# Last local attention of a twelve-layer kernel: order of the last quarter's units, and who multiplies what

## The reference, cut to what matters

```python
def _L3_attn_ref(x, w_qkvw, w_out):
    H = 16; G = 4; DIM = 128; HD = DIM // H // G          # HD = 2
    B, S, dim = x.shape
    qkvw = x @ w_qkvw
    chunks = jnp.split(qkvw, G, axis=-1)
    subs = [jnp.split(t, G, axis=-1) for t in chunks]
    q = jnp.concatenate([subs[i][0] for i in range(4)], axis=0)   # k: [1], v: [2], w: [3]
    ...
    q, k, v = (shp(q), shp(k), shp(v))        # reshape(B*G, H, -1, HD).swapaxes(1, 2)
    w = w.reshape(B * G, H, -1, HD)
    scores = q @ k.swapaxes(-2, -1) * HD ** (-0.5)
    attn = jax.nn.softmax(scores, axis=-1)
    o = (attn @ v).swapaxes(1, 2).reshape(B, S, dim)
    return o * w.reshape(B, S, dim) @ w_out
...
x = x + _L3_attn_ref(_layernorm(x, axis=-1), L3_attn_w_qkvw, L3_attn_w_out)
x = x + _L3_ffn_ref(_layernorm(x, axis=-1), ...)
```

## Time and profile before

| | us |
|---|---|
| median of 3 runs | 2057.41 (2051.45 to 2058.58) |
| profiled execution | 2055.21 |
| its span | 2053.4 |
| TensorE matmul busy | 1747.0 (85%) |
| VectorE busy | 1340.8 (65%) |
| ScalarE busy | 1045.8 (51%) |
| GpSimd busy | 904.9 (44%) |

### The profile page before, as it was taken

One profiled execution on the slowest core, in us unless ns is written; L12 is line 12 of the kernel. 1 busy time (PEld: TensorE's weight loads), 2 busy tenths in 40 slices (PEclk: granted clock), 3 DMA queues, 4 the chain that ended last, 5 costly groups with the idle time before them and its releaser, 6 DMA issues.

```text
span 2053.4 us, 50642 instructions
## 1 busy us (share of the span) xinstructions
PE 1747.0 (85%) x20238; PEld 1177.5 (57%) x20238; DVE 1340.8 (65%) x3578; ACT 1045.8 (51%) x2709; POOL 904.9 (44%) x1088
## 2 busy tenths in 40 slices
PE   7678999999988789998888879999999997447596
PEld 4323556566664555654566656776676764125496
DVE  6799996576675565455672277656877876666622
ACT  4445665487873652224532346666666753115243
POOL 2343554555551523320514152326767578433543
PEclk9878999999999999999978999999999998766598
DMA  9000000100008100034014301000000000040197
GB/s 362 1 1 0 0 1 1 77 5 5 4 5 348 67 4 0 1 153 197 3 68 133 110 22 42 22 22 20 13 25 19 11 12 1 10 155 30 57 308 231
DMA packets 60429, 130.68 MB, mean 64 GB/s; under 512 B 16714, under 2 KB 38941, under 8 KB 54561
## 3 DMA queue, kind: packets, MB, share of 16 engines
q1 hardware_dynamic: 56896, 121.32, 16.5%
q0 software_dynamic: 3296, 6.12, 0.9%
HBM read 107.97 MB, written 20.12 MB: 62 GB/s over the span
## 4 chain that ended last, share of the span: by engine, by line
PE 55%; DVE 20%; issue 9%; ACT 7%; DMA 4%; POOL 4%; SPq 1%; POOLq 1%; DVEq 0%; ACTq 0%
PE PS L3321 4%; PE PS L2516 4%; PE PS L424 3%; PE PS L3368 3%; PE PS L3353 2%; PE PS L3352 2%; DMA arena<-in_ctx 2%; PE PS L3310 2%; PE PS L460 2%; PE PS L1521 2%; PE PS L2316 2%; PE PS L4328 2%; PE PS L4319 2%; PE PS L1497 2%; PE PS L1082 1%
## 5 line engine op out<-in xcount | busy, mean ns | idle before, releaser
L321 POOL TENSOR_TENSOR arena<-arena 128x4 f32<-128x4 f32 (+3 forms) x109 | 118.7, 1089 | 347.4 <-DVE arena L264 225.9
L1655 POOL TENSOR_TENSOR arena<-arena 128x128 f32<-128x128 f32 x448 | 164.4, 404 | 53.0 <-PE PS L1703 15.6
L3436 ACT ACTIVATE arena<-PS,arena 128x289 f32<-128x289 f32 x256 | 127.6, 503 | 73.2 <-DVE arena L3550 72.8
L3550 DVE TENSOR_REDUCE arena<-PS 128x1 f32<-128x289 f32 x256 | 113.5, 454 | 71.9 <-PE PS L3321 67.8
L3321 PE MATMUL PS<-arena 128*128 128x289 f32 x512 | 150.6, 417 | 10.4 <-ACT arena L3436 7.5
L1258 POOL TENSOR_TENSOR arena<-arena 128x512 f32<-128x512 f32 x64 | 83.9, 1311 | 109.8 <-DVE arena L1403 109.8
L1610 ACT COPY arena<-PS 32x128 f32<-32x128 f32 x384 | 99.5, 259 | 21.8 <-PE PS L1511 17.7
L3321 PEld LDWEIGHTS PS<-arena 128*128 128x128 f32 x512 | 87.4, 191 | 34.5 <-ACT arena L3436 16.8
L3279 POOL TENSOR_TENSOR arena<-arena 128x1024 f32<-128x1024 f32 x14 | 33.0, 2355 | 159.8 <-ACT arena L3427 159.8
L3564 DVE TENSOR_TENSOR arena<-PS,arena 128x580 f32<-128x580 f32 x128 | 97.6, 762 | 4.4
L368 PE MATMUL PS<-arena 128*128 128x512 f32 x166 | 89.9, 677 | 9.5 <-DVEq L4635 8.7
(11 more groups left out here) (471 smaller groups left out, 4768.6 us busy)
## 6 DMA issues: line engine op xcount, KB each, us to landing
arena<-in_ctx SPq DMA_DIRECT2D x32, 1091.0 KB, 10.2
arena<-in_f_w SPq DMA_DIRECT2D x39, 514.0 KB, 5.5
arena<-in_ctx SPq DMA_DIRECT2D x16, 834.0 KB, 16.3
lists<-arena SPq DMA_DIRECT2D x8, 1040.0 KB, 10.8
arena<-in_f_w SPq DMA_DIRECT2D x32, 256.0 KB, 2.9
arena<-in_ctx SPq DMA_DIRECT2D x16, 512.0 KB, 3.9
arena<-in_mid SPq DMA_DIRECT2D x1, 3796.5 KB, 12.4
arena<-in_late SPq DMA_DIRECT2D x1, 3204.0 KB, 11.4
```

What stands on the lines that cost most here:

```text
L321: e.tensor_tensor(x, x, half.broadcast_to(list(x.shape)), ALU.pow).then_inc(*T.done("norm_root", tag))
L1655: k = e.tensor_tensor(dst[:, b], spread(src[:, b, :], [P, HG, S], 1), spread(self.g.C["headmask"], [P, HG, S], 2), ALU.mult)
L3436: e.activation(self.weights(n, k, 0, UL), PS[:, self.score_bank(n, k), 0:UL], ACT.Exp, bias=self.st[:, h, k:k + 1], accum_out=self.st[:, h ...
L3550: e.tensor_reduce(self.st[:, n % 2, k:k + 1], PS[:, self.score_bank(n, k), 0:UL], AXX, ALU.max, negate=True).then_inc(*T.done("k3_least", ...
```

## The change

In quarter 3's part and what is interleaved with it:

1. GpSimd issues both end products right after the first two of its six remaining passes; the other four follow them.
2. VectorE issues `products(0)`, `products(1)`, then both residual adds, then the mix of unit 10; the norm statistics of quarters 0 and 1 are taken out of `residual` and come later, one after that mix and one after `maxima(0)`; the mix of unit 11 comes before `maxima(1)` instead of after it.
3. VectorE's two products read the query features from PSUM, where TensorE left them, instead of from `z`.
4. TensorE adds the products of both end units before it subtracts either's maxima.
5. End unit 1's second weighing moves from VectorE to GpSimd, so GpSimd does three of the four; the exponential into PSUM is not made for unit 1.
6. At the end VectorE adds and begins quarter 2, applies the norm of quarters 0 to 2, and only then adds and begins quarter 3.
7. `mix_dve` waits for its own engine's total, which otherwise nothing orders ahead of it.

```diff
+    def feature_of(self, z, r, f, lo, n):
+        return z.rearrange("p h (r j e) -> p r e j h", r=4, e=2)[:, r, f, lo:lo + n, :]
     def feature(self, q, r, f, lo, n):
-        return self.z[q % 2].rearrange("p h (r j e) -> p r e j h", r=4, e=2)[:, r, f, lo:lo + n, :]
+        return self.feature_of(self.z[q % 2], r, f, lo, n)
@@ pe
         add_products(0)
+        add_products(1)
         subtract(0)
-        add_products(1)
         subtract(1)
@@ act
-            e.activation(banks, banks, ACT.Exp, scale=float(2 ** -0.5)).then_inc(*T.done("m3_exp_again", u))
+            if u == 0:
+                e.activation(banks, banks, ACT.Exp, scale=float(2 ** -0.5)).then_inc(*T.done("m3_exp_again", u))
@@ pool
-            e.tensor_tensor(self.by_four(self.vp[u][:, 0, :]), self.ex[u].rearrange("p j (h g) -> p j h g", g=self.NP),
-                            spread(self.at_end(u, 2, 0), self.wide_end, 2), ALU.mult).then_inc(*T.done("m3_weighed", ("end", u)))
+            for f in range(1 + u):
+                m = e.tensor_tensor(self.by_four(self.vp[u][:, f, :]), self.ex[u].rearrange("p j (h g) -> p j h g", g=self.NP),
+                                    spread(self.at_end(u, 2, f), self.wide_end, 2), ALU.mult)
+            m.then_inc(*T.done("m3_weighed", ("end", u)))
 
         self.root_pool(e, T, NT - 1)
-        for what, U in rest[:-2]:
+        for what, U in rest[:2]:
             self.pass_pool(e, T, what, U)
         products(0)
-        for what, U in rest[-2:]:
+        products(1)
+        for what, U in rest[2:]:
             self.pass_pool(e, T, what, U)
-        products(1)
@@ mix_dve
+        for w in T.due(("m3_total", U)):
+            e.wait_ge(*w)
         e.reciprocal(total, total).then_inc(*T.step())
@@ dve
         def products(u):
+            made = PS[:, 4:8, :].rearrange("p b (a d) -> p (b a) d", a=4)
             for w in T.due(*features):
                 e.wait_ge(*w)
-            e.tensor_tensor(self.pb[u].rearrange("p j (h g) -> p j h g", g=NP), spread(self.at_end(u, 0, 1), self.wide_end, 3),
+            e.tensor_tensor(self.pb[u].rearrange("p j (h g) -> p j h g", g=NP),
+                            spread(self.feature_of(made, 0, 1, JE * u, JE), self.wide_end, 3),
                             spread(self.at_end(u, 1, 1), self.wide_end, 2), ALU.mult).then_inc(*T.done("m3_second_dve", ("end", u)))
@@ weigh
             e.reciprocal(total, total).then_inc(*T.step())
+            if u:
+                return
@@ residual
             e.tensor_tensor(x, four(PS[:, b, :]), x, ALU.add).then_inc(*T.done("m3_added", q))
+
+        def begin(q):
             for w in T.due(("m3_added", q)):
                 e.wait_ge(*w)
             self.after.begin_dve(e, T, q)
@@ order on VectorE
         products(0)
-        for q in range(2):
-            residual(q, q)
         products(1)
+        residual(0, 0)
+        residual(1, 1)
         self.mix_dve(e, T, mixes[0], self.mixed)
+        begin(0)
+        self.total_dve(e, T, totals[1])
         maxima(0)
-        self.total_dve(e, T, totals[1])
+        begin(1)
+        self.mix_dve(e, T, mixes[1], self.mixed)
         maxima(1)
-        self.mix_dve(e, T, mixes[1], self.mixed)
         weigh(0)
         weigh(1)
         mix(0)
         mix(1)
-        for q in range(2, NQ):
-            residual(q, q - 2)
-            self.after.begin_rows_dve(e, T, q - 2)
-        self.after.begin_rows_dve(e, T, NQ - 2)
+        residual(2, 0)
+        begin(2)
+        for q in range(NQ - 1):
+            self.after.begin_rows_dve(e, T, q)
+        residual(3, 1)
+        begin(3)
```

## The result

| | before | after |
|---|---|---|
| median, us | 2054.43 (2048.52 to 2058.58) | 2031.64 (2023.45 to 2033.89) |
| ratio to before, 95% interval | | 0.988 (0.986 to 0.990) |
| span of the profiled execution, us | 2053.4 | 2030.7 |

The change makes the kernel 22.8 us faster; 21.3 were forecast, and 2036 us against 2031.64. From here on I read one **stretch**: from the end of VectorE's last copy of features to the end of its last norm application for quarter 3. I read its length and not its start, because the start moves from execution to execution. Before it was 97.8 us (1732.01 + 0.69 to 1830.47; TensorE's turn of the norm's rows starts 0.06 later), after it is 73.9 (1733.92 to 1807.81): 23.9 us saved. The features were done 1.2 us later than in the trace of before, and behind the stretch 222.9 us follow in both; 23.9 - 1.2 is the 22.7 by which the spans differ.

A forecast was written before the change was run, and what follows sets the result against it. Bound: a latency chain across engines from the last feature copy to the last layer's norm. Mix 1 ending 16.4 us earlier plus 4.9 of norm application gives 21.3; 2057.4 - 21.3 = 2036 us, range 2029 to 2046.

The forecast's parts named there:

- the subtraction of unit 1: TensorE, end unit 1: starts at 1763.0 after 3.1 us idle, taken as cold at 6.3 us; warm would be 3.7.
- rival A: TensorE's subtraction for unit 1 runs at full clock, 2.6 us less: 2033.5 us; chance 0.58 together with the forecast.
- the forecast's own case: Path as laid out, 2036 us, including unit 1's subtraction running warm at 2033.5; chance 0.58 together.
- the added wait: Wait in `mix_dve` for VectorE's own total: nothing to 0.1 us each for ten units; 0 taken, 1 for the range.
- The products: VectorE's end products with query features from PSUM: 3.5 us each, leaving GpSimd's two at 4.85 each undisturbed.
- C: End products: VectorE's PSUM-reading ones still exclude GpSimd's, both pairs in series add 7.0 us: 2043; chance 0.09.
- The moved weighing: Unit 1's second weighing puts 5.5 us on GpSimd's path, takes 3.5 off VectorE's; GpSimd ends at 1782.3, after VectorE's mix 0.
- The norm application: End of VectorE's list: norm of two quarters no longer stands behind the last add, saving 4.9 us.
- The statistics: VectorE's norm statistics of quarters 0 and 1, moved later: 2.0 us each, one stall of 1.6 in place of 5.1.
- B: VectorE's last multiplications of unit 11's mix wait behind GpSimd's weighing, unit 1 comes 6.5 us later: 2042.5; chance 0.18.
- D: VectorE reads the query pattern from PSUM slowly, making the kernel slower; at 22 us more per product, 2069; chance 0.04.
- E: Behind the shortened stretch, in the last layer's head stream or quarter 3's rows, half the gain is lost: 2047; chance 0.11.

## Why the prediction was right

The path was the one laid out, and nearly every stop on it was met. In us after the features:

| | laid out | measured |
|---|---|---|
| GpSimd's second product ends | 9.8 | 9.9 |
| additions end | 23.5 | 23.7 |
| small operation stalled by GpSimd | 1.6 | 1.4 |
| maxima of unit 1 end | 30.3 | 30.3 |
| exponential of unit 1 ends | 38.5 | 35.9 |
| mix 1 ends | 55.1 | 52.6 |
| add of quarter 3 starts | 69.2 | 66.6 |
| last norm application ends | 76.5 | 73.9 |

**The mis-sized term** is the subtraction of unit 1: I took 6.3 for a cold start, it took 3.71 at a granted clock of 1.00. That is rival A, kept in the forecast's own case, 2.6 us, and the whole difference between 21.3 and 23.9. I had chosen between the two prices by the idle time ahead (3.02 us, laid out as 3.1), and that did not decide it. The other 1.2, by which the features came later, can't be laid to the added wait: with it the features were done at 1731.5 and 1732.8, without it at 1730.5 and 1736.0, four kernels on one chip, and four kernels with it on another had them between 1725.4 and 1732.9, though nothing ahead of that point differs among those four. A cost of the wait below this scatter is not ruled out. By the same scatter it is partly luck that the two profiled executions differ by 22.7 us, so near the 22.8 of the medians and the 21.3 forecast; the 23.9 of the stretch is the firmer figure.

**The products** were right as a mechanism and as a size (7.34 for two at 3.5 laid out); undoing them showed C at 82.6 in the stretch, 8.7 more, where I had 7.0. **The moved weighing** was right: GpSimd's two, not VectorE, end last, by 1.2 us. **The norm application** was worth 5.0 (4.9 laid out). **The statistics** I had treated as the removal of one stall; undone they cost 5.6, and neither the three further stalls nor TensorE's second cold start at full length stood in my sum for that. It did not matter for the forecast, which followed the new order, but it did for what each part is worth. Two more pieces of part 2, the second product ahead of the residual adds and the mix of unit 11 ahead of the maxima of unit 1, were not undone singly; what they are worth is not shown.

**Rivals.** B did not happen, by 1.2 us against a margin laid out as 1.0; its price was about right: the 6.5 laid out are the delay that provokes it and the wait, and provoked these were 2.3 and 4.8. The other 2.2 of the 9.3 are a slower subtraction, which the forecast had in its own case already. D did not: the query pattern from PSUM cost 3.67 us a product, near the 3.52 of the row it was taken from. E did not, at the 10 us forecast for it: 222.9 us follow the stretch before and after. The eight other kernels of the two groups at 2055 us have 222.8 to 225.6, so a loss under some 3 us could not be seen.

The Trainium skill's rule in "SBUF — State Buffer", section "Who interferes with whom", that a VectorE instruction with two SBUF inputs contends with GpSimd's reads and one with at most one does not, is borne out from both sides: VectorE's products with one SBUF input ran free (7.34 beside 9.79), with two they took turns (11.85 beside 16.56), and in the order of issue a 0.29 us instruction waited 5.09.

## What to carry to other kernels

When work on several in-order engines is reordered, lay out the new order on the old trace row by row and put a start beside every instruction; parts cannot be priced one at a time. Undone singly, the six parts cost 8.7, 2.5, 10.1, 5.6, 5.0 and 8.2, 40.1 us together for a gain of 23.9, and put in singly one gave 3.8 and another took 7.0 (5.7 without GpSimd's later start). Next to a GpSimd instruction of several us, look for every small VectorE instruction with two SBUF operands or in a scalar form, and note its margin: 1.2 us of it separate this kernel from one that is some 7 us slower (9.3 less the 2.3 of work put in).

## What the runs showed of the hardware

The clock that TensorE was granted for unit 1's subtraction did not follow the idle time ahead of it. Its eight instructions took 3.71 us (granted clock 1.00, that is 2.4 GHz) after 2.38, 2.85, 2.94, 3.01, 3.02 and 3.05 us of idle, 5.40 (0.68 on average over them) after 2.39, 3.36 and 3.93, and 5.88 (0.62) after 10.39. The one at 2.39 is the kernel with TensorE's order undone. A cold subtraction earlier does not explain it, since the kernel before had one too and got 1.00 after 2.38. Unit 1's additions show the same: they started at 0.50 (1.2 GHz) after 2.67 us of idle in the kernel before, and at 1.00 after 3.43 in the same kernel with the PSUM operand alone. Idle time alone, on which I had chosen between the two prices, was not enough to choose; what else decides stays open.

Reading TensorE's output from PSUM with the strided, repeated pattern cost VectorE nothing: 3.67 us a product (7.34 for two) against 3.68 for one from SBUF. And GpSimd's instruction with the root, 1.6 us, did not hold VectorE's norm application of two SBUF operands (L295 and L300 took 1.14 for four beside it); only its products of 1024 and 2048 words were seen to hold VectorE. The reason stays open.
